# The opening of a fused kernel: loads, casts and residuals reordered across four engines

## The chip, the cores and the metric

The kernel runs on one core of one Trainium2 chip. The metric is the device time of one execution in microseconds; the profile's "span" is the time from the first to the last instruction of the profiled execution.

## The reference

```python
# x: 128 samples, 32 channels, 512 positions; all float32
def cond(x, c, weight, c_weight, bias):        # grouped convolution, 9 taps, 4 groups
    out = conv(x, weight, padding=4, groups=4)
    return out + (c @ c_weight.T)[:, :, None] + bias[None, :, None]

def ffn(y, base_W, base_b, router_W, router_b, A, B, expert_map):
    base_out = y @ base_W.T + base_b                       # 512 -> 512
    probs = softmax(y @ router_W.T + router_b)             # 15 routes
    topk_p, topk_i = top_k(probs, 8)
    w = sum of topk_p per expert, by expert_map[topk_i]    # 8 experts
    h = y @ A                                              # 8 experts x rank 16
    return base_out + ((h * w) @ B) * 2.0

out = x + ffn(cond(x, ...), ...)
```

## The kernel before

**Tiles.** The 4096 rows (sample, channel) of 512 positions are worked through as 32 tiles of 128 rows (4 samples, Q). Two tiles make a pair (8 samples), and the convolution is done by pairs, in two halves of 16 channels (`HALVES`); a unit is one half of one pair.

**Precision.** Every float32 operand of a matmul is split into a high part (`x_hi`, `wide_hi`, `y_hi`, `conv_hi`, a cast on ScalarE) and the residual (`x_lo`, `wide_lo`, ..., a subtraction on VectorE or GpSimd). A product is then three matmuls: high by high, the weight's residual by high, high by the data's residual. A residual reads two tensors in SBUF.

**Work of one tile t.** `conv` gives sums in PSUM; VectorE adds the conditioning (`condition`) and transposes (`turn`) into `y`; ScalarE casts (`y_high`); GpSimd makes `y_lo` (`y_low`). TensorE's `linear` multiplies y by the wide weights (`wide_sb`: 4 runs of 656 columns: A, router and base weights) into two PSUM banks, 400 columns in the first (FRONT_BANK) and 256 in the second. VectorE's `choose` (logits, best, top 8), `mark` and `weigh` make the routed hidden rows `hw`; TensorE turns `hw` (`turn_hw`), ScalarE and VectorE split it (`hw_high`, `hw_low`), TensorE's `up` adds it onto the sums, and VectorE's `add_out` adds x and the bias. `bias_rows` and `terms_low` are GpSimd's own work for each tile.

**Steps.** Every engine has its own function `step(t, k, p)` which is unrolled for the first 4 and last 8 tiles and looped between. In TensorE's step t the order is: front of `linear(t)`, `turn_hw(t-1)`, three runs of the second bank, `up(t-1)`, the last run, `conv(t)`. In VectorE's step t: `condition(t)`, `turn(t+2)`, `difference(t+5)`, `choose(t)`, `hw_low(t-1)`, `mark(t)`, `weigh(t)`, `add_out(t-1)`. The front of `linear(t)` waits for `out_added` of tile t-2, since it writes the same banks. Each engine executes its list in order, and a waiting instruction holds all behind it.

**Opening.** Tiles 0 to 3 (two pairs, `START`) don't use the looped convolution with its terms, but `conv_first` on plain blocks of x. The first pair is handled in its two tiles (a = 0, 1) and the second pair as a whole (`conv_second_pair`), after `linear(0)`. The first looped convolution, `conv(0)`, makes unit 4; its operands come from `difference`, `terms_high` and `terms_low`, and `conv_sum` is a weight that only it and its followers need. The tile `cond_sb` holds the conditioning; its weights come from HBM already repeated for each of the 8 output rows. `keep_warm` issues matmuls on zeros whose result nobody reads. DMAs are issued from SP's queue in the order written, apart from `conv_w` (ScalarE's) and the two that are read by all partitions, `expert_map` and `biases` (GpSimd's).

## Time and profile before

| | |
|---|---|
| time, median of 3 runs | 201.25 us (201.13 to 201.28) |
| the profiled execution's own time | 201.2 us |
| its span | 199.4 us |
| mean granted TensorE clock | 0.988 |
| TensorE busy | 189.7 us, 95% |
| VectorE busy | 163.1 us, 82% |
| GpSimd busy | 143.0 us, 72% |
| ScalarE busy | 76.5 us, 38% |

The profiled execution took 201.2 us, 1.8 us more than its span and 0.05 us less than the median. The busy times are sums over the whole span. All of the change lies in the opening, roughly the first 32 us, so the rows below are nearly all from there.

### The profile page before, as it was taken

Reading aid. Unit: us, or ns where it says so; the run is one execution under the profiler, and the core shown is the slowest. Engines: PE = TensorE matmul, PEld = TensorE weight load, DVE = VectorE, ACT = ScalarE, POOL = GpSimd, SP = SyncE. Lnnn points to the kernel's source line nnn. Section 1 sums busy time; section 2 is a strip of 40 time slices with the busy share of each in tenths; the row PEclk is TensorE's granted clock in tenths of the full one; section 3 lists DMA queues with packets and bytes.
Section 4 is the critical chain, followed back from the end, with each engine's and each line's share of the span. In section 5 each row is a group of like instructions: output and inputs, shape, how many; then the busy total and the mean of one; then the engine's idle time right before and its main releaser. Section 6 shows DMA issues by size and latency. Waiting matters only on the chain.

```text
span 199.4 us, 4327 instructions
## 1 busy us (share of the span) xinstructions
PE 189.7 (95%) x1300; PEld 181.7 (91%) x1300; DVE 163.1 (82%) x548; ACT 76.5 (38%) x196; POOL 143.0 (72%) x113
## 2 busy tenths in 40 slices
PE   7788699999999999999999999999999999998993
PEld 2667499999999999999999999999999999997992
DVE  1399898888898889898888889888988888775673
ACT  5164253444444343334444434333444443222210
POOL 5359989777777778877777777887777777943520
PEclk9999979999999999999999999999999999999998
DMA  7894054334445544434445544444343333333312
GB/s 168 281 393 161 16 144 141 119 121 133 130 159 165 159 159 139 144 117 135 131 130 156 159 159 159 137 146 121 125 153 118 100 105 108 105 105 110 105 53 105
DMA packets 18955, 27.78 MB, mean 139 GB/s; under 512 B 2112, under 2 KB 10176, under 8 KB 18944
## 3 DMA queue, kind: packets, MB, share of 16 engines
q1 hardware_dynamic: 18544, 26.98, 41.9%
q0 software_dynamic: 112, 0.28, 0.7%
q10 hardware_dynamic: 288, 0.39, 0.7%
q8 instruction: 5, 0.08, 0.2%
q14 instruction: 6, 0.05, 0.1%
HBM read 19.25 MB, written 8.39 MB: 139 GB/s over the span
## 4 chain that ended last, share of the span: by engine, by line
PE 83%; POOL 4%; DVE 4%; DMA 4%; issue 2%; ACT 1%; SPq 1%; DVEq 0%; ACTq 0%
PE wide_ps L496 54%; PE conv_banks L479 15%; PE wide_ps L520 10%; DMA x_in<-x_start 4%; POOL is_expert L430 2%; PE hwt_bank L507 2%; PE conv_banks L496 1%; POOL terms_lo L414 1%; DVE xr L612 1%; POOL y_lo L420 1%; DVE y_rows L617 1%; POOL map_f L427 0%; PE conv_banks L520 0%; DVE y L701 0%; SPq L251 0%
## 5 line engine op out<-in xcount | busy, mean ns | idle before, releaser
L496 PE MATMUL wide_ps<-wide_hi,y_hi 128*128 128x400 f32 (+1 forms) x248 | 80.8, 330 | 1.0 <-DVE xr L612 0.9
L496 PE MATMUL wide_ps<-wide_lo,y_hi 128*128 128x400 f32 (+1 forms) x248 | 76.6, 313 | 0.5 <-DVE wide_lo L221 0.5
L496 PE MATMUL wide_ps<-wide_hi,y_lo 128*128 128x400 f32 (+1 forms) x248 | 76.7, 314 | 0.0
L414 POOL TENSOR_TENSOR terms_lo<-terms,terms_hi 128x768 fp32r<-128x768 f32 x28 | 51.7, 1847 | 30.9 <-ACT terms_hi L336 30.9
L496 PEld LDWEIGHTS wide_ps<-wide_hi,y_hi 128*128 128x128 f32 x248 | 46.8, 190 | 3.5 <-issue 1.2
L496 PEld LDWEIGHTS wide_ps<-wide_lo,y_hi 128*128 128x128 f32 x248 | 46.8, 190 | 0.8 <-DVE wide_lo L221 0.8
L496 PEld LDWEIGHTS wide_ps<-wide_hi,y_lo 128*128 128x128 f32 x248 | 46.5, 189 | 0.0
L409 POOL TENSOR_TENSOR xr<-xr,biases_sb 128x512 f32<-128x512 f32 x32 | 41.5, 1296 | 6.2 <-DMA xr<-x_rows 6.2
L420 POOL TENSOR_TENSOR y_lo<-y,y_hi 128x512 fp32r<-128x512 f32 x32 | 41.4, 1293 | 3.3 <-ACT y_hi L343 3.3
L350 ACT ACTIVATE hw_hi<-hwt_bank 128x128 fp32r<-128x128 f32 x31 | 8.6, 278 | 82.5 <-PE hwt_bank L507 82.5
L343 ACT ACTIVATE y_hi<-y 128x512 fp32r<-128x512 f32 x32 | 20.3, 633 | 17.8 <-PE wide_ps L496 17.0
L479 PE MATMUL conv_banks<-terms_hi,conv_hi 128*128 128x256 f32 x84 | 23.7, 283 | 1.9 <-POOL terms_lo L414 1.9
L336 ACT ACTIVATE terms_hi<-terms 128x768 fp32r<-128x768 f32 x28 | 23.2, 829 | 2.6 <-DVE terms L642 2.6
L479 PE MATMUL conv_banks<-terms_lo,conv_hi 128*128 128x256 f32 x84 | 23.9, 285 | 0.0
L479 PE MATMUL conv_banks<-terms_hi,conv_lo 128*128 128x256 f32 x84 | 23.8, 283 | 0.0
L701 DVE STREAM_TRANSPOSE y<-y_rows 128x512 f32<-128x512 f32 x32 | 22.6, 708 | 1.1
L633 DVE TENSOR_TENSOR y_rows<-conv_banks,common 128x512 f32<-128x512 f32 x28 | 19.4, 692 | 2.9
L612 DVE TENSOR_TENSOR xr<-wide_ps,xr 128x512 f32<-128x512 f32 x30 | 20.4, 682 | 0.5 <-PE wide_ps L520 0.3
L642 DVE TENSOR_TENSOR terms<-even,odd_bank 128x256 f32<-128x256 f32 x56 | 20.0, 395 | 0.0
L479 PEld LDWEIGHTS conv_banks<-terms_hi,conv_hi 128*128 128x128 f32 x84 | 16.0, 191 | 2.3 <-issue 2.3
L479 PEld LDWEIGHTS conv_banks<-terms_hi,conv_lo 128*128 128x128 f32 x84 | 16.1, 191 | 0.0
L479 PEld LDWEIGHTS conv_banks<-terms_lo,conv_hi 128*128 128x128 f32 x84 | 16.0, 191 | 0.0
(93 smaller groups left out, 265.7 us busy)
## 6 DMA issues: line engine op xcount, KB each, us to landing
xr<-x_rows SPq DMA_DIRECT2D x32, 256.0 KB, 2.7
out<-xr SPq DMA_DIRECT2D x31, 256.0 KB, 2.0
even<-x_even SPq DMA_DIRECT2D x28, 132.0 KB, 2.5
...
```

What stands on the lines that cost most here:

```text
L336: nc.scalar.activation(terms_hi[i % 2][:, :, :, :], terms[i][:, :, :, :], ACT.Copy)\
L343: nc.scalar.activation(y_hi[k % 2][:, :, :], y[k % 2][:, :, :], ACT.Copy)\
L409: nc.gpsimd.tensor_tensor(xr[k][:, :], xr[k][:, :], base_b_sb[:, :], ALU.add)\
L414: nc.gpsimd.tensor_tensor(terms_lo[i % 2][:, :, :, :], terms[i][:, :, :, :], terms_hi[i % 2][:, :, :, :].bitcast(F32), ALU.subtract)\
L420: nc.gpsimd.tensor_tensor(y_lo[k % 2][:, :, :], y[k % 2][:, :, :], y_hi[k % 2][:, :, :].bitcast(F32), ALU.subtract)\
L479: mm = nc.tensor.matmul(sums, w[:, h, j, :], a[i][:, j, :, :], start=w is conv_hi and a is terms_hi, stop=a is terms_lo)
L496: mm = nc.tensor.matmul(sums_of(t, k)[:, b, 0:columns[1] - columns[0]], a[k % 2][:, r, :], w[:, r, columns[0]:columns[1]], start=r == 0 an ...
L520: mm = nc.tensor.matmul(sums_of(t, k)[:, b, first:first + HALF], a[k % 2][:, :], w[:, b * HALF:(b + 1) * HALF], start=False, stop=True, sk ...
L612: nc.vector.tensor_tensor(rows, linear_sums(t, k), rows, ALU.add)\
L633: nc.vector.tensor_tensor(y_rows[i][:, h, :, :].rearrange("p n (a k) -> p a n k", a=2), own_ps, common[:, :, :].unsqueeze(1).to_broadcast( ...
L642: d = nc.vector.tensor_tensor(terms[i][:, j, :, :], even[i][:, :, j:j + MK], odd_ps, ALU.subtract)
L701: nc.vector.transpose(y[k % 2][:, :, :].rearrange("p r (n h o) -> p h n r o", n=Q, h=HALVES), y_rows[(k // 2) % 2][:, :, own, :]).then_inc ...
```

## The change

The loads are issued in another order and in other pieces: the x blocks of tile 0, run 0 of the wide weights, the x blocks of tile 1, runs 1, 2 and 3, the second pair. `cond` goes to ScalarE's queue with 83 KB in place of 193 KB, and GpSimd repeats its weights for the 8 output rows. `biases` goes from GpSimd's queue to SP's. All x_hi of the opening are ScalarE's; x_lo of tile 0 stays with VectorE and those of tile 1 and the second pair go to GpSimd; all four wide_lo and y_lo of tile 0 are VectorE's; `is_expert` is one VectorE instruction in place of eight of GpSimd. `add_condition` writes its rows in order and reads PSUM with a step of two, where it read in order and wrote with a step. On VectorE, `choose`, `mark` and `weigh` of tile 0 now come ahead of the rows of the second pair, and `up_lo` after them; on TensorE, `conv(0)` now comes behind the front of `linear(1)`, and the three products of `conv_first` are issued in the order in which their operands come.

```diff
@@ sync
-            sync.dma_start(x_in[0][:, :, 0:Q, :], x_start[0, :, :, 0:Q, :])\
-                .then_inc(x_first_in, 16)
-            sync.dma_start(cond_in_sb[:, :], cond).then_inc(cond_in, 16)
-            sync.dma_start(x_in[0][:, :, Q:, :], x_start[0, :, :, Q:, :]).then_inc(x_second_in, 16)
-            for r in range(0, RUNS, 2):
-                sync.dma_start(wide_sb[:, r:r + 2, :], wide_w[:, r:r + 2, :])\
-                    .then_inc(wide_in[r // 2], 16)
-            sync.dma_start(x_in[1][:, :, :, :], x_start[1]).then_inc(x_third_in, 16)
+            sync.dma_start(x_in[0][:, :, :, :], x_first[0]).then_inc(x_loaded[0], 16)
+            load_wide(0)
+            sync.dma_start(x_in[1][:, :, :, :], x_first[1]).then_inc(x_loaded[1], 16)
+            load_wide(1)
+            load_wide(2)
+            load_wide(3)
+            sync.dma_start(x_in[2][:, :, :, :], x_pair).then_inc(x_loaded[2], 16)
             load_terms(0, 0)
+            sync.dma_start(biases_sb[:, :], biases.partition_broadcast(P)).then_inc(biases_in, 16)
+            load_terms(1, 1)
             sync.dma_start(up_sb[:, :], up_w).then_inc(up_in, 16)
-            load_terms(1, 1)
@@ tensor
+            for a in range(PAIR // Q):
+                sums = first_ps if a == 0 else conv_ps[:, :, Q:, :]
+                pe.wait_ge(x_hi_ready, a + 1)
+                for h in range(HALVES):
+                    conv_first(sums[:, h, :, :], a, h, (X_HIGH,))
                 for h in range(HALVES):
                     if a == 0:
                         pe.wait_ge(conv_lo_ready, h + 1)
+                    conv_first(sums[:, h, :, :], a, h, (X_W_REST,))
                 if a == 0:
                     ...
+                for h in range(HALVES):
+                    pe.wait_ge(x_lo_ready[a], h + 1)
+                    mm = conv_first(sums[:, h, :, :], a, h, (X_REST,))
+                mm.then_inc(first_done, 1)
@@ tensor, first_step and step
-                pe.wait_ge(y_lo_ready, 1)
+                for r in runs[:RUNS // 2]:
+                    pe.wait_ge(wide_lo_ready, r + 1)
+                    linear(0, 0, (r,), products=(W_REST,))
+                pe.wait_ge(y_lo_first, 1)
                 linear(0, 0, runs, products=(Y_REST,), last=(RUNS - 1, W_REST))
...
                     linear(t, k, runs, (FRONT_BANK,)).then_inc(front_done, 1)
+                    if isinstance(t, int) and t == 1:
+                        conv(0, 0, 0)
                     turn_hw(t - 1, k - 1)
@@ vector, add_condition
-                    rows.rearrange("p n (a k) -> p n k a", a=2),
-                    sums.rearrange("p n (k a) -> p n k a", a=2),
-                    c.unsqueeze(2).unsqueeze(3).to_broadcast([P, batches, MK, 2]), ALU.add)\
+                    rows.rearrange("p n (a k) -> p n a k", a=2),
+                    sums.rearrange("p n (k a) -> p n a k", a=2),
+                    c.unsqueeze(2).unsqueeze(3).to_broadcast([P, batches, 2, MK]), ALU.add)\
@@ vector, step 0
+                if isinstance(t, int) and t == 0:
+                    dve.wait_ge(up_hi_ready, 1)
+                    nc.vector.scalar_tensor_tensor(out=up_lo[:, :], in0=up_sb[:, :], ...)
+                    return
```

The lists below are the engines' programs in order, each instruction with its output, inputs and size. First VectorE in the opening, before: from the residual of tile 1's x blocks (`x_lo0`, here a part of the pair's tile) to the transpose of tile 2.

```order
L605 TENSOR_TENSOR x_lo0<-x_in0,x_hi0 128x2x260
L731 TENSOR_SCALAR cond_sb<-odd_bank,cond_in_sb 128x128 x2
L617 TENSOR_TENSOR y_rows0<-wide_ps0,cond_sb 128x4x32x2 x2
L701 STREAM_TRANSPOSE y0<-y_rows0 128x2x4x4x16
L617 TENSOR_TENSOR y_rows0<-conv_banks,cond_sb 128x4x32x2 x2
L701 STREAM_TRANSPOSE y1<-y_rows0 128x2x4x4x16
L221 TENSOR_TENSOR wide_lo<-wide_sb,wide_hi 128x656 x3
L743 SCALAR_TENSOR_TENSOR up_lo<-up_sb,up_hi 128x512
L605 TENSOR_TENSOR x_lo1<-x_in1,x_hi1 128x520 x2
L642 TENSOR_TENSOR terms0<-even0,odd_bank 128x256 x2
L617 TENSOR_TENSOR y_rows1<-conv_banks,cond_sb 128x8x32x2 x2
L701 STREAM_TRANSPOSE y0<-y_rows1 128x2x4x4x16
```

The same place after the change, from `wide_lo` of run 0 to the first operation of `choose`, tile 0 (`logits0`).

```order
L752 TENSOR_TENSOR wide_lo<-wide_sb,wide_hi 128x656
L766 TENSOR_TENSOR cond_sb<-odd_bank,cond_in_sb 128x256
L642 TENSOR_TENSOR y_rows0<-wide_ps0,cond_sb 128x256 x2
L726 STREAM_TRANSPOSE y0<-y_rows0 128x2x4x4x16
L752 TENSOR_TENSOR wide_lo<-wide_sb,wide_hi 128x656
L773 TENSOR_TENSOR y_lo0<-y0,y_hi0 128x512
L752 TENSOR_TENSOR wide_lo<-wide_sb,wide_hi 128x656 x2
L642 TENSOR_TENSOR y_rows0<-conv_banks,cond_sb 128x256 x2
L726 STREAM_TRANSPOSE y1<-y_rows0 128x2x4x4x16
L781 TENSOR_TENSOR is_expert<-map_f,expert_ids 128x120
L667 TENSOR_TENSOR terms0<-even0,odd_bank 128x256 x2
L674 TENSOR_TENSOR logits0<-wide_ps0,biases_sb 128x15
```

The two large x_lo and up_lo are gone from here, and a fourth wide_lo, y_lo0 and is_expert have come. The first wide_lo stands ahead of cond_sb and of tile 0's rows, and the logits of tile 0 stand ahead of y_rows1 (the second pair).

GpSimd from behind the memsets to the first bias rows, before:

```order
L397 DMA map_i<-expert_map 128x15
L399 TENSOR_TENSOR conv_sum<-conv_sb 128x256
L402 TENSOR_TENSOR conv_lo<-conv_sum,conv_hi 128x2x128
L405 DMA biases_sb<-biases 128x527
L221 TENSOR_TENSOR wide_lo<-wide_sb,wide_hi 128x656
L420 TENSOR_TENSOR y_lo0<-y0,y_hi0 128x512
L427 CAST map_f<-map_i 128x15
L430 TENSOR_SCALAR is_expert<-map_f 128x15 x8
L420 TENSOR_TENSOR y_lo1<-y1,y_hi1 128x512
L414 TENSOR_TENSOR terms_lo0<-terms0,terms_hi0 128x768
L409 TENSOR_TENSOR xr0<-xr0,biases_sb 128x512
```

and after:

```order
L406 DMA map_i<-expert_map 128x15
L408 MEMSET expert_ids 128x1 x8
L410 COPY cond_w_sb<-cond_in_sb 128x256
L224 TENSOR_TENSOR x_lo1<-x_in1,x_hi1 128x260 x2
L417 CAST map_f<-map_i 128x15
L419 TENSOR_TENSOR conv_sum<-conv_sb 128x256
L224 TENSOR_TENSOR x_lo2<-x_in2,x_hi2 128x520 x2
L438 TENSOR_TENSOR y_lo1<-y1,y_hi1 128x512
L445 TENSOR_TENSOR conv_lo<-conv_sum,conv_hi 128x2x128
L432 TENSOR_TENSOR terms_lo0<-terms0,terms_hi0 128x768
L427 TENSOR_TENSOR xr0<-xr0,biases_sb 128x512
```

GpSimd has lost wide_lo, y_lo0, eight is_expert and one DMA issue, and has got eight small memsets, the copy of the conditioning weights and four x_lo, two of 128x260 and two of 128x520.

ScalarE from the weight casts of the convolution on, before:

```order
L303 ACTIVATE conv_hi<-conv_sb 128x256 x2
L306 ACTIVATE conv_hi<-conv_sum 128x2x128
L309 ACTIVATE x_hi0<-x_in0 128x2x260
L315 ACTIVATE wide_hi<-wide_sb 128x656 x2
L343 ACTIVATE y_hi0<-y0 128x512
L315 ACTIVATE wide_hi<-wide_sb 128x656 x2
L357 ACTIVATE x_hi1<-x_in1 128x1040
L343 ACTIVATE y_hi1<-y1 128x512
L330 COPY odd_bank<-terms0 128x256
L362 ACTIVATE up_hi<-up_sb 128x512
```

and after:

```order
L309 ACTIVATE conv_hi<-conv_sb 128x256 x2
L313 ACTIVATE x_hi0<-x_in0 128x520
L319 ACTIVATE wide_hi<-wide_sb 128x656
L313 ACTIVATE x_hi1<-x_in1 128x520
L319 ACTIVATE wide_hi<-wide_sb 128x656 x2
L347 ACTIVATE y_hi0<-y0 128x512
L319 ACTIVATE wide_hi<-wide_sb 128x656
L313 ACTIVATE x_hi2<-x_in2 128x1040
L365 ACTIVATE conv_hi<-conv_sum 128x2x128
L334 COPY odd_bank<-terms0 128x256
L347 ACTIVATE y_hi1<-y1 128x512
```

The cast `wide_hi` of run 0 now stands between the casts of tile 0's and tile 1's x blocks, and the cast of conv_sum has moved behind all of them.

## Rows read from the trace of the kernel before

**Rows 1.** Windows: stretch, length, busy us of PE, PEld, DVE, ACT, POOL, PEclk, DMA share, GB/s.

```profile
4.00:6.00 2.00, 1.33 (x4) 0.15 (x1) 1.75 (x3) 0.62 (x2) 1.47 (x3) 1.00 0.96 112
8.00:10.00 2.00, 2.00 (x11) 1.85 (x9) 0.09 (x1) 0.64 (x1) 0.00 (x0) 1.00 1.01 416
24.06:27.47 3.41, 3.41 (x15) 3.39 (x14) 2.94 (x14) 1.96 (x5) 2.31 (x2) 0.50 0.59 155
60.00:115.00 55.00, 55.00 (x400) 54.35 (x399) 48.79 (x170) 22.82 (x60) 43.27 (x31) 1.00 0.47 144
```

**Rows 2.** Timeline, 20 to 33 us: start, us, engine, instruction [idle before <-releaser].

```profile
20.41 1.13 DVE L617 TENSOR_TENSOR y_rows<-conv_banks,cond_sb 128x512 f32<-128x512 f32 x1 [0.51 <-PE conv_banks L457]
...
21.83 1.05 DVE L617 TENSOR_TENSOR y_rows<-conv_banks,cond_sb 128x512 f32<-128x512 f32 x1 [0.28 <-PE conv_banks L457]
22.97 0.71 DVE L701 STREAM_TRANSPOSE y<-y_rows 128x512 f32<-128x512 f32 x1
...
23.66 0.36 PE L479 MATMUL conv_banks<-terms_hi,conv_hi 128*128 128x256 f32 x1 [1.87 <-POOL terms_lo L414]
...
24.24 0.16 DVE L649 TENSOR_TENSOR logits<-wide_ps,biases_sb 128x15 f32<-128x15 f32 x1
...
25.35 0.28 DVE L673 TENSOR_TENSOR spread<-is_expert,wide_ps 128x120 f32<-128x120 f32 x1
...
26.33 0.41 DVE L628 TENSOR_TENSOR common<-conv_banks,cond_sb 128x256 f32<-128x256 f32 x1
...
26.85 0.69 DVE L633 TENSOR_TENSOR y_rows<-conv_banks,common 128x512 f32<-128x512 f32 x1
...
27.46 0.70 DVE L701 STREAM_TRANSPOSE y<-y_rows 128x512 f32<-128x512 f32 x1
...
29.22 0.29 DVE L712 TENSOR_TENSOR hw_lo<-hwt_bank,hw_hi 128x128 fp32r<-128x128 f32 x1
...
31.16 0.69 DVE L612 TENSOR_TENSOR xr<-wide_ps,xr 128x512 f32<-128x512 f32 x1 [0.19 <-issue]
...
32.00 0.42 PE L496 MATMUL wide_ps<-wide_hi,y_hi 128*128 128x400 f32 x1
```

**Rows 3.** Timeline, 9 to 20 us.

```profile
9.24 0.64 ACT L309 ACTIVATE x_hi<-x_in 128x520 fp32r<-128x520 f32 x1 [4.53 <-DMA x_in<-x_start]
9.91 0.70 DVE L605 TENSOR_TENSOR x_lo<-x_in,x_hi 128x520 fp32r<-128x520 f32 x1 [3.32 <-ACT x_hi L309]
10.53 0.60 DVE L731 TENSOR_SCALAR cond_sb<-odd_bank,cond_in_sb 128x128 f32<-128x128 f32 x2
...
10.89 1.40 ACT L315 ACTIVATE wide_hi<-wide_sb 128x656 fp32r<-128x656 f32 x2 [1.01 <-DMA wide_sb<-wide_w]
...
11.16 1.13 DVE L617 TENSOR_TENSOR y_rows<-wide_ps,cond_sb 128x256 f32<-128x256 f32 x2
...
17.94 1.30 DVE L605 TENSOR_TENSOR x_lo<-x_in,x_hi 128x520 fp32r<-128x520 f32 x2
```

**Rows 4.** Timeline, 3 to 14 us, GpSimd.

```profile
3.54 0.72 POOL L399 TENSOR_TENSOR conv_sum<-conv_sb 128x256 f32<-128x256 f32 x1 [0.62 <-DMA conv_sb<-conv_w]
...
4.79 1.18 POOL L402 TENSOR_TENSOR conv_lo<-conv_sum,conv_hi 128x256 fp32r<-128x256 f32 x1 [0.53 <-ACT conv_hi L306]
...
13.78 1.30 POOL L420 TENSOR_TENSOR y_lo<-y,y_hi 128x512 fp32r<-128x512 f32 x1 [0.47 <-ACT y_hi L343]
```

**Rows 5.** Instructions of lines L724, L221 and L315: ns min/median/max, first and last start.

```profile
L724 DVE TENSOR_TENSOR conv_lo<-conv_sb,conv_hi x2: 412/680/947, 5.3 to 6.2; 128x256 fp32r<-128x256 f32 x2
...
L221 DVE TENSOR_TENSOR wide_lo<-wide_sb,wide_hi x3: 828/829/1097, 14.7 to 16.4; 128x656 fp32r<-128x656 f32 x3
...
L315 ACT ACTIVATE wide_hi<-wide_sb x4: 736/738/754, 10.9 to 14.3; 128x656 fp32r<-128x656 f32 x4
```

**Rows 6.** Tiles wide_sb, then map_i: from issue to landing, min/median/max.

```profile
DMA to landing us min/median/max: 8.2/9.0/9.9
...
DMA to landing us min/median/max: 6.5/6.5/6.5
```

More of the change, by code:

```diff
@@ L131, in build @@
         cond_in = sem("cond_in")
-        wide_in = [sem(f"wide_in{i}") for i in range(RUNS // 2)]
+        cond_w_ready = sem("cond_w_ready")
+        wide_in = [sem(f"wide_in{i}") for i in range(RUNS)]
         up_in = sem("up_in")
@@ L176, in build @@
         y_hi_ready = sem("y_hi_ready")
+        y_lo_first = sem("y_lo_first")
         y_lo_ready = sem("y_lo_ready")
@@ L421, in y_low @@
                                         y_hi[k % 2][:, :, :].bitcast(F32), ALU.subtract)\
[L422 to L432 removed]
+                    .then_inc(y_lo_ready, tiles)
+            y_low(1, 1, 2)
+            pool.wait_ge(conv_sum_hi_ready, 1)
+            nc.gpsimd.tensor_tensor(conv_lo[:, :, BLOCKS, :], conv_sum[:, :, :],
+                                    conv_hi[:, :, BLOCKS, :].bitcast(F32), ALU.subtract)\
+                .then_inc(conv_sum_lo_ready, 1)
             terms_low(FIRST_UNIT, 0)
@@ L484, in conv @@
                 mm.then_inc(conv_done, 1)
+            X_HIGH, X_W_REST, X_REST = (conv_hi, x_hi), (conv_lo, x_hi), (conv_hi, x_lo)
             FRONT_BANK, NEXT_BANK = 0, 1
@@ L740, in _ @@
                 turn(a, a)
-            split_wide(dve, nc.vector, range(1, RUNS))
-            dve.wait_ge(up_hi_ready, 1)
-            nc.vector.scalar_tensor_tensor(out=up_lo[:, :], in0=up_sb[:, :], scalar=LORA_SCALE,
-                                           in1=up_hi[:, :].bitcast(F32), op0=ALU.mult,
-                                           op1=ALU.subtract).then_inc(up_lo_ready, 1)
-            dve.wait_ge(x_hi_ready, 2)
-            for h in range(HALVES):
-                x_low_first(1, (every, h, every, every))
-            difference(FIRST_UNIT, 0)
+            wide_low(0)
+            dve.wait_ge(cond_summed, 1)
+            nc.vector.tensor_tensor(cond_sb[:, :, :], cond_ps,
+                                    conv_b_sb.unsqueeze(2).to_broadcast([P, HALVES, N]), ALU.add)\
+                .then_inc(cond_biased, 1)
+            dve.wait_ge(cond_biased, 1)
+            first_rows(0, first_ps)
+            wide_low(1)
+            dve.wait_ge(y_hi_ready, 1)
+            nc.vector.tensor_tensor(y_lo[0][:, :, :], y[0][:, :, :],
+                                    y_hi[0][:, :, :].bitcast(F32), ALU.subtract)\
+                .then_inc(y_lo_first, 1)
+            wide_low(2)
+            wide_low(3)
+            first_rows(1, conv_ps[:, :, Q:, :])
+            dve.wait_ge(map_ready, 1)
+            dve.wait_ge(ids_ready, E)
+            nc.vector.tensor_tensor(is_expert[:, :, :],
+                                    map_f[:, :].unsqueeze(1).to_broadcast([P, E, ROUTES]),
+                                    expert_ids[:, :].unsqueeze(2).to_broadcast([P, E, ROUTES]),
+                                    ALU.is_equal).then_inc(is_expert_ready, 1)
+            difference(FIRST_UNIT, 0)
+            dve.wait_ge(biases_in, 16)
+            choose(0, 0)
+            mark(0, 0)
+            dve.wait_ge(is_expert_ready, 1)
+            weigh(0, 0)
             for h in range(HALVES):
@@ L805 @@
     blocks = blocks.reshape(N // PAIR, P, HALVES, PAIR, MI)
+    first = blocks[0].reshape(P, HALVES, 2, Q, MI).transpose(2, 0, 1, 3, 4)
     units = blocks[START:].transpose(0, 2, 1, 3, 4).reshape(-1, P, PAIR, MI)
@@ L831 @@
     given = {
-        "x_start": blocks[:START],
+        "x_first": first,
+        "x_pair": blocks[1],
         "x_even": units[..., 0::2],
```

170 lines of the change are left out of this document (83 added, 87 removed).

## The prediction

> **What bounds the kernel now.** The page's totals (the table above) have TensorE busy for 95% of the span and VectorE for 82%. Next the windows: from 60 to 115 us TensorE is busy for 55.00 of 55 us at full clock [rows 1]. The change leaves those steps alone, so a gain must show as an earlier start of the steady part. As its mark I take the start of linear(2), 32.00 us [rows 2]; 167.4 us of the span follow it.
>
> What ends last before that mark is read from the timeline, backwards. TensorE starts linear(2) at 32.00, right behind VectorE's add_out of tile 0 (31.16 + 0.69 = 31.85) [rows 2]. That in turn ends an unbroken list of VectorE: common of step 1 starts at 26.33, hw_lo at 29.22, add_out at 31.16. TensorE looks worse off than VectorE: it waited 1.87 us for terms_lo before conv(0) at 23.66 [rows 2], and ran at half clock from 24.06 to 27.47 [rows 1]. But both were hidden, for VectorE reached the logits of tile 0 only at 24.24 and common at 26.33. So the path is VectorE's list from 9.91 (x_lo of tile 1, released by a cast at 9.24, released by a DMA [rows 3]) to 26.33: 16.42 us, in which it idled only 0.51 + 0.28 = 0.79 us, for the sums of the second pair (ahead of 20.41 and 21.83 [rows 2]). I call the start of common of step 1 C1. Before, C1 = 26.33 and linear(2) = C1 + 5.67.
>
> **The change on VectorE's list, in costs from start to start.**
> - Gone: x_lo of tile 1, 10.53 - 9.91 = 0.62; x_lo of the second pair, 1.22 for two (17.94 onwards; 1.30 busy, the next starts 0.08 before the end as elsewhere [rows 3]). Sum 1.84.
> - Gone: the waits of 0.79. The routes of tile 0 now stand there, 26.33 - 24.24 = 2.09 [rows 2], and cover them. Without that cover they would be back.
> - cond_sb: 11.16 - 10.53 = 0.63 [rows 3] becomes one instruction of 256 columns from PSUM like common, 26.85 - 26.33 = 0.52 [rows 2]. Saves 0.11.
> - add_condition: two of 128x256 took 1.13 us [rows 3], so four some 2.25; the two of 128x512 took 1.13 and 22.97 - 21.83 = 1.14 [rows 2]. Instructions from PSUM that write in order take 0.41 for 256 columns (common) and 27.46 - 26.85 = 0.61 for 512 [rows 2]. No row shows a read of PSUM with a step. Bounds: as now, saving 0, or as those. I take the second, nearest in all else: (2.25 - 4 x 0.41) + (2.27 - 2 x 0.61) = 0.61 + 1.05 = 1.66.
> - Added: wide_lo of run 0, 0.83 (the median [rows 5]); y_lo of tile 0, 0.64 (512 columns are 0.69 busy, as in add_out, less the same overlap); is_expert, 0.28, as the 120-column spread [rows 2]. Sum 1.75. up_lo, the differences and the transposes only change place.
>
> **The price of giving x_lo to GpSimd.** Conv_lo is twice the same instruction on VectorE and took 412 and 947 ns [rows 5]; the long one ran while GpSimd was in its own conv_lo, 4.79 to 5.97, which took 1.18 us, where conv_sum of the same size took 0.72 [rows 4]. The longest wide_lo, 1097 ns against 828, was the first, from 14.7 [rows 5], while GpSimd's y_lo ran until 13.78 + 1.30 = 15.08 [rows 4]. So these two engines hold each other up when each reads two SBUF tensors. After the change, x_lo of the second pair (two of about 1.30 us, as y_lo of like size [rows 4]) comes up for GpSimd near 15 us, amid wide_lo 2 and 3 on VectorE. Bounds: nothing, if VectorE always comes first; 2.5 us, if both halves do. I take one half, for the two queues should alternate: 1.20 us. The loss of 0.27 in a wide_lo is kept, now against conv_sum.
>
> The Trainium skill (SBUF — State Buffer, "Who interferes with whom") says that VectorE with two SBUF inputs and GpSimd reading SBUF fully block each other, whoever issues first. That speaks against this edit. Where the rows alone, taken as each engine losing half of an overlap, would charge 0.6 us here, by the rule it is a whole GpSimd instruction, or two.
>
> Sum: 16.42 - 1.84 - 0.79 - 0.11 - 1.66 + 1.75 + 1.20 = 14.97 us from the start of the list to C1.
>
> **When the list starts.** wide_lo of run 0 is first, so it waits for run 0's DMA and cast. The DMAs are crippled early: 112 GB/s in 4 to 6 us at a busy share of 0.96, 416 GB/s in 8 to 10 [rows 1]. Meanwhile the small map_i load is out, 6.5 us on its way [rows 6]; it stays where it is. The second x piece landed at 9.2, the first wide piece at 10.9 [rows 3]. Up to the second x piece 256 + 260 + 193 + 260 = 969 KB were asked for; up to run 0 it will be 256 + 83 + 260 + 328 = 927 KB. The 42 KB are 0.1 us at 416 GB/s, so run 0 lands at about 9.1; its cast takes 0.74 [rows 5] and the list starts at 9.87, almost as before. Bounds: without the slow stretch 927 KB at 416 GB/s from the 2 us at which data begins to flow would land at 4.4; at the other end 11.4, below.
>
> C1 = 9.87 + 14.97 = 24.84, against 26.33.
>
> **What else could hold C1?** Following the same costs down the list, wide_lo 3 ends at 17.3, tile 1's rows at 18.1 and its transpose at 18.7, and the routes at 21.9. TensorE does the second pair's matmuls behind those rows and is done by 21, within the routes. Conv(0) needs terms_lo: ScalarE's y_hi1 19.4, then GpSimd's y_lo1 20.7, conv_lo (0.7 to 1.2) 21.6, terms_lo (1.8) 23.4; its first part is done at 23.8, 1 us to spare. hw_lo follows C1 by 2.89 us as before, for the same steps precede it [rows 2]. TensorE will idle at up(0) instead, 1.5 to 2.5 us that cost nothing by themselves. So linear(2) = 24.84 + 5.67 = 30.51. The span becomes 197.9, the profiled time 199.7, and against the median 201.25 - 1.49 = **199.75 us**. The keep_warm matmuls ahead of linear(0) (7, now 4) lie where TensorE waits for y_hi of tile 0 and count for nothing; without that wait fewer could only help.
>
> **The rivals.**
> - *The clock.* Before, a half-clock stretch of 3.41 us [rows 1] followed TensorE's wait of 1.87 us [rows 2]. After the change such a wait stands at up(0), about 25.5 to 27.7. The stretch costs half of itself, 1.7 us of work; some 0.85 us is free between the end of conv(1) and linear(2). So 0.85 us is paid if it falls before that mark, 1.7 at most if across it: 200.6, at worst 201.45. For it: this wait. Against: it is broken by up(0)'s first products. Chance 0.2.
> - *The rows stay dear.* If a read with a step costs as much as the write did, 1.66 us of the gain goes: 201.4, no change. Chance 0.12.
> - *The slow DMA stretch shrinks.* If run 0 lands a us or more earlier, the list starts as much earlier, until later weights bind: 198.0 to 198.8. Chance 0.15. For it: VectorE's cast of tile 0's x, at 4.2, falls into the slow stretch and goes. Against: map_i goes out as before. The Trainium skill (SBUF — State Buffer, "SBUF: two separate sides") says that a float32 copy on VectorE keeps GpSimd from writing the descriptors of its own DMA; by that rule map_i would be over sooner. No row here separates this.
> - *Slower: run 0 lands late.* A wide piece took up to 9.9 us from issue [rows 6]. Issued second, at about 1.5, run 0 would then land at 11.4, 2.3 us later than I take; as it stands ahead of cond_sb, all of VectorE's list moves: 199.75 + 2.3 = 202.05. It decides from a landing after 11.0. For it: it lies in the slow stretch. Against: only small loads are ahead of it. Chance 0.12; other losses that end above 201.65 (both halves of x_lo ahead of wide_lo together with half clock) 0.08.
> - The forecast, 199.1 to 200.4, has the remaining 0.33.
>
> **Numbers.** The range for 8 in 10 reaches from the early landing, 198.1, to a little past the late one's threshold, 201.9. About 0.2%, or 0.4 us, is what this kernel's timing can tell from no change. Faster by more: the forecast 0.33, the early DMA 0.15, most of the clock's 0.2 (0.15): 0.63. Same: 0.12 + 0.05 = 0.17. Slower: 0.20.
>
> **What would show it.** C1, the first common, near 24.8; linear(2) near 30.5; wide_lo of run 0 beginning near 9.9 with VectorE idle ahead of it; y_rows at 0.41 and 0.69 us; one of the last two wide_lo lengthened by about 1.2 us beside GpSimd's x_lo; no gap on VectorE between that and C1; TensorE waiting at up(0). The forecast is wrong if VectorE is not what linear(2) waits for, if run 0 lands far from 9.1, or if the granted clock is 0.5 when linear(2) starts.

## The result, and the profile after

The changed kernel takes 198.26 us in the median of 4 runs (197.58 to 198.88), the kernel before 201.26 beside it: ratio 0.985, 95% interval 0.981 to 0.988. The gain is 3.0 us where 1.5 were forecast; 198.26 lies at the lower edge of the range (198.1 to 201.9), and in size it is the rival "the slow DMA stretch shrinks": its condition, run 0 landing a us or more earlier, came true, though the stretch did not shrink. The same kernel measured once more (e18 below) took 197.70 (197.46 to 198.00) beside 201.37.

VectorE's list in the opening, in the timeline of the profiled execution (start, duration, in brackets the idle time ahead and what ended it). These rows answer to [rows 2, 3].

```profile
6.91 0.83 DVE L752 TENSOR_TENSOR wide_lo<-wide_sb,wide_hi 128x656 fp32r<-128x656 f32 x1
9.05 0.42 DVE L766 TENSOR_TENSOR cond_sb<-odd_bank,cond_in_sb 128x256 f32<-128x256 f32 x1 [1.32 <-PE odd_bank L557]
9.98 0.76 DVE L642 TENSOR_TENSOR y_rows<-wide_ps,cond_sb 128x256 f32<-128x256 f32 x2 [0.50 <-PE wide_ps L471]
...
11.41 0.80 DVE L752 TENSOR_TENSOR wide_lo<-wide_sb,wide_hi 128x656 fp32r<-128x656 f32 x1
12.18 0.69 DVE L773 TENSOR_TENSOR y_lo<-y,y_hi 128x512 fp32r<-128x512 f32 x1
12.79 1.59 DVE L752 TENSOR_TENSOR wide_lo<-wide_sb,wide_hi 128x656 fp32r<-128x656 f32 x2
...
15.71 1.24 DVE L781 TENSOR_TENSOR is_expert<-map_f,expert_ids 128x120 f32<-128x120 f32 x1
...
19.70 1.28 DVE L642 TENSOR_TENSOR y_rows<-conv_banks,cond_sb 128x512 f32<-128x512 f32 x2
...
22.88 0.41 DVE L653 TENSOR_TENSOR common<-conv_banks,cond_sb 128x256 f32<-128x256 f32 x1
```

C1, the start of `common` of step 1, is at 22.88 us, 3.45 earlier than the 26.33 of before [rows 2]. Two things differ from the forecast's list at its head: wide_lo of run 0 is long done, and VectorE then idles 1.32 and 0.50 us for TensorE. GpSimd beside it:

```profile
7.29 1.74 POOL L224 TENSOR_TENSOR x_lo<-x_in,x_hi 128x260 fp32r<-128x260 f32 x2 [0.92 <-ACT x_hi L313]
...
13.93 2.89 POOL L224 TENSOR_TENSOR x_lo<-x_in,x_hi 128x520 fp32r<-128x520 f32 x2 [3.15 <-ACT x_hi L313]
```

TensorE's timeline: first convolution, then from up(0) to linear(2).

```profile
1.32 4.02 PE L465 MATMUL wide_ps<-zeros 128*128 128x512 bf16 x9 [1.32 <-POOL zeros L400]
6.09 1.22 PE L471 MATMUL wide_ps<-x_hi,conv_hi 128*128 128x256 f32 x4 [0.74 <-ACT x_hi L313]
7.11 1.05 PE L471 MATMUL wide_ps<-x_hi,conv_lo 128*128 128x256 f32 x4
7.96 1.05 PE L557 MATMUL odd_bank<-cond_in_sb,cond_w_sb 128*128 128x128 f32 x4
...
24.38 0.48 PE L535 MATMUL wide_ps<-up_hi,hw_hi 128*128 128x256 f32 x2 [0.75 <-ACT hw_hi L354]
...
26.09 0.50 PE L535 MATMUL wide_ps<-up_hi,hw_lo 128*128 128x256 f32 x2 [1.00 <-DVE hw_lo L737]
...
27.37 0.42 PE L493 MATMUL conv_banks<-terms_hi,conv_lo 128*128 128x256 f32 x1
27.59 0.41 PE L493 MATMUL conv_banks<-terms_lo,conv_hi 128*128 128x256 f32 x1
...
28.52 0.67 PE L511 MATMUL wide_ps<-wide_hi,y_hi 128*128 128x400 f32 x1
```

Linear(2) starts at 28.52, C1 + 5.64 (before: + 5.67). But the span is 197.1, so 168.6 us follow it where 167.4 did before. The windows show why, and how the loads fared; the last three columns are granted clock, DMA share and GB/s, as in [rows 1].

```profile
4.00:6.00 2.00, 1.35 (x4) 0.16 (x2) 0.76 (x2) 1.21 (x4) 0.04 (x1) 1.00 1.06 393
6.00:8.00 2.00, 1.91 (x9) 1.91 (x10) 1.67 (x3) 1.20 (x3) 1.08 (x2) 1.00 0.97 148
8.00:10.00 2.00, 2.00 (x11) 2.00 (x11) 0.44 (x2) 0.32 (x1) 1.15 (x3) 1.00 0.93 359
...
26.00:28.00 2.00, 1.91 (x12) 1.91 (x13) 1.63 (x9) 1.67 (x4) 2.00 (x3) 0.77 0.50 141
28.00:30.00 2.00, 2.00 (x9) 1.84 (x8) 1.86 (x4) 0.00 (x0) 2.00 (x2) 0.50 0.36 135
```

The slow DMA stretch did not go: it came at 6 to 8 us (148 GB/s) instead of 4 to 6 (112 [rows 1]). Run 0 landed ahead of it, at 5.74, and the second x piece as it began, at 6.48 (ScalarE casts them at 5.94 and 6.58 without a wait); run 1 landed behind it, at 9.66. Two signs that the forecast had named against itself are there: run 0 landed far from 9.1, and the granted clock was 0.5 when linear(2) started.

### The profile page after: what moved, and what is told of

It reads as the page before. It is cut to its first block, busy times and chain, and to the rows that moved or that the text cites. A ratio compares the mean times of both kernels' runs of the same rounds, so it can differ in the third digit from the quotient of the medians.

```text
span 197.1 us, 4329 instructions
## 1 busy us (share of the span) xinstructions
PE 189.0 (96%) x1297; PEld 181.9 (92%) x1297; DVE 161.1 (82%) x547; ACT 77.0 (39%) x197; POOL 139.4 (71%) x115
## 4 chain that ended last, share of the span: by engine, by line
PE 84%; DVE 9%; issue 2%; DMA 2%; ACT 1%; DVEq 0%; ACTq 0%
PE wide_ps L511 53%; PE conv_banks L493 15%; PE wide_ps L535 10%; DMA conv_sb<-conv_w 2%; PE hwt_bank L522 2%; PE wide_ps L471 1%; PE conv_banks L511 1%; DVE y_rows L642 1%; DVE wide_lo L752 1%; DVE y L726 1%; DVE terms L667 1%; DVE xr L637 1%; DVE spread L698 0%; DVE expert_w L702 0%; PE odd_bank L557 0%
## 5 line engine op out<-in xcount | busy, mean ns | idle before, releaser
L438 POOL TENSOR_TENSOR y_lo<-y,y_hi 128x512 fp32r<-128x512 f32 x31 | 40.2, 1296 | 3.4 <-ACT y_hi L347 3.4
```

The costliest lines, as they stand in the source:

```text
L438: nc.gpsimd.tensor_tensor(y_lo[k % 2][:, :, :], y[k % 2][:, :, :], y_hi[k % 2][:, :, :].bitcast(F32), ALU.subtract)\
```

## The experiments

There are eighteen runs; C1 and the start of the first y_rows are from each profiled execution. The kernel before measured 201.0 to 201.4 us in the medians beside them, so that differences under some 0.4 us between rows of the table are not shown by the times alone; the ratio is to the kernel before beside the run.

| run | time, us (range) | ratio, 95% interval | first y_rows | C1 |
|---|---|---|---|---|
| before | 201.26 | 1 | 11.16 | 26.33 |
| changed | 198.26 (197.58-198.88) | 0.981-0.988 | 9.98 | 22.88 |
| e1 run 0 behind x | 197.96 (197.55-198.37) | 0.980-0.986 | 8.20 | 23.02 |
| e5 map first | 197.41 (196.91-197.87) | 0.977-0.984 | 9.89 | 22.79 |
| e9 warm-up 10 | 197.93 (197.44-198.60) | 0.981-0.988 | 8.22 | 22.69 |
| e17 cond last | 197.97 (197.28-199.03) | 0.980-0.986 | 8.60 | 22.33 |
| e18 changed again | 197.70 (197.46-198.00) | 0.979-0.984 | 8.11 | 22.87 |
| e4 before, new loads | 201.84 (201.33-202.28) | 1.001-1.004 | 11.88 | 27.14 |
| e6 before, map late | 200.71 (199.77-200.83) | 0.994-0.998 | 10.79 | 25.91 |
| e14 before, rows | 200.99 (200.34-201.36) | 0.997-1.001 | 11.04 | 25.55 |
| e15 before, rows and routes | 199.30 (198.93-199.84) | 0.988-0.994 | 11.37 | 24.39 |
| e2 old rows | 199.12 (198.15-199.70) | 0.983-0.991 | 9.87 | 23.88 |
| e10 pair on VectorE | 199.68 (198.62-200.02) | 0.986-0.993 | 9.97 | 24.18 |
| e11 rows ahead of routes | 199.63 (199.48-199.90) | 0.989-0.994 | 8.24 | 24.66 |
| e7 is_expert early | 197.33 (196.95-198.40) | 0.978-0.984 | 9.73 | 22.40 |
| e8 warm at up(0) | 197.29 (197.19-197.55) | 0.978-0.984 | 8.00 | 22.15 |
| e3 map late | 196.67 (196.12-198.82) | 0.974-0.986 | 8.03 | 21.08 |
| e12 together | 198.01 (197.92-198.47) | 0.982-0.987 | 8.17 | 22.87 |
| e13 together, second | 197.14 (196.92-197.24) | 0.977-0.983 | 8.18 | 21.91 |
| e16 map late, warm | 196.36 (196.22-196.66) | 0.973-0.980 | 8.10 | 21.17 |

**What sets the head of the list.** e1 swaps two loads of the changed kernel, e4 gives the kernel before the new order of loads.

```diff
 e1
-            load_wide(0)
             sync.dma_start(x_in[1][:, :, :, :], x_first[1]).then_inc(x_loaded[1], 16)
+            load_wide(0)
 e4: x piece 1, run 0, x piece 2, runs 1 to 3 one by one; cond on ScalarE's queue
```

> The changed kernel with one edit: run 0 of the weights is issued behind the second x piece instead of ahead of it. Theory (the list's head): the gain beyond the forecast came from run 0 landing before the slow DMA stretch. Behind it, run 0 lands when run 1 did, at about 9.7 us; its cast ends at 10.4, wide_lo of run 0 starts at 10.45 and cond_sb at 11.3 instead of 9.05, so the first common goes from 22.88 to about 25 and the time from 198.3 to about 200.4. Rival (the list itself got shorter, its head does not matter): the first common moves by under 0.5 us and the time by under 0.5.

> The kernel before with the changed kernel's load order only (run 0 second, then the second x piece, each run by itself, cond on ScalarE's queue). Theory (the load order alone brings the early start): the second x piece lands by 7 us instead of 9.2, x_lo of tile 1 starts near 7.3 instead of 9.91, and the first y_rows come at about 10 instead of 11.16, held by TensorE's first matmuls; the first common comes 1.2 to 1.6 us earlier and the time is 199.7 to 200.2. Rival (the early landing is owed to something else in the change, as to what GpSimd or VectorE do in the opening): x and run 0 land as late as before and the time stays at 201.2.

Both expectations failed, and so did the reading that the place of run 0 in the queue matters. In e1 run 0 still landed as the slow stretch began (cast at 6.20). In e4 it landed in the stretch, at 7.09, and the second x piece behind it: ScalarE waited 5.11 us and cast the piece at 9.96, later than before. Up to that piece e4 asks for 256 + 260 + 328 + 260 + 193 = 1297 KB, the changed kernel, with 83 KB of cond, for 1187. That is 0.3 us at 400 GB/s and does not by itself explain 3.5 us. The issue times on SyncE's queue say more (before and e4, then the changed kernel; GpSimd issues expert_map at 2.17 or 2.16 in all three):

```profile
2.08 0.55 SPq L254 DMA_DIRECT2D x_in<-x_start  x1
2.08 0.55 SPq L256 DMA_DIRECT2D x_in<-x_start  x1
1.66 0.42 SPq L264 DMA_DIRECT2D x_in<-x_first  x1
```

The second x piece, issued at 2.08, landed at 9.22 and 9.94; issued at 1.66 it landed at 6.48. Run 1 of the changed kernel, issued at 2.13, landed at 9.66. So what was issued 0.5 us or more ahead of expert_map came in ahead of the stretch or in it, and what was issued within 0.1 us of it came behind. In the changed kernel one issue follows the other every 0.44 to 0.47 us, before and in e4 every 0.59 to 0.73. No run changes the issue times alone, so this is what the traces agree on and not shown as the cause. e5 and e6 move the load of expert_map, which I suspected of making the stretch:

```diff
 e5
             nc.gpsimd.memset(zeros[:, :], 0.0).then_inc(zeros_ready, 1)
+            pool.dma_start(map_i[:, :], expert_map.partition_broadcast(P)).then_inc(map_in, 16)
 e6, in before.py, behind the load of x_in[1]
+            sync.dma_start(map_i[:, :], expert_map.partition_broadcast(P)).then_inc(map_in, 16)
```

> The changed kernel with the small load of expert_map issued about 1 us earlier, as GpSimd's second instruction. Theory (that load makes the slow DMA stretch, and the stretch comes where the load stands among the loads issued): the slow stretch begins before 5 us instead of at about 6, the second x piece and run 0 land in or behind it as in the kernel before (after 7.5 us), the first common is 24 or later instead of 22.9 and the time 199.2 to 200.5. Rival (the stretch comes at a set time after the loads begin, whatever the order): it stays at 6 to 8 us and the time stays within 0.5 us of the changed kernel's 198.3.

> The kernel before with the load of expert_map issued by SyncE behind the second pair's x, nothing else. Theory (the kernel before lost its start to the slow DMA stretch): no slow stretch; the second x piece lands near 5.5 us instead of 9.2; TensorE's first matmuls, from 6.4, then set the pace, so the first y_rows come at 8.5 to 9.7 instead of 11.16; the first common comes 1.5 to 2.5 us earlier than 26.33 and the time falls to 198.8 to 199.8. Rival (other loads or engines hold the list anyway, as when run pairs land late): under 0.8 us gained.

The windows of e5 have the stretch a us earlier:

```profile
5.00:6.00 1.00, 0.35 (x2) 0.01 (x1) 0.79 (x3) 1.00 (x4) 0.17 (x1) 1.00 0.82 74
6.00:7.00 1.00, 1.00 (x4) 1.00 (x5) 1.00 (x3) 0.58 (x1) 0.23 (x1) 1.00 0.77 252
```

So the first half of the theory stands: the stretch follows that load. The packets of GpSimd's queue agree: they begin at 4.4 us before, 5.2 in e4, 5.8 in the changed kernel and 4.9 in e5, and the stretch begins with them; why they came later in the changed kernel than before, from the same issue time, stays open. The theory's price does not stand: the second x piece was cast at 7.52 instead of 6.58, and C1 stayed (22.79). e6 has no stretch there and gained 0.4 us of C1, not 1.5 to 2.5. Its timeline says what else held the kernel before:

```profile
7.11 0.70 DVE L605 TENSOR_TENSOR x_lo<-x_in,x_hi 128x520 fp32r<-128x520 f32 x1 [0.57 <-ACT x_hi L310]
10.14 0.61 DVE L731 TENSOR_SCALAR cond_sb<-odd_bank,cond_in_sb 128x128 f32<-128x128 f32 x2 [2.33 <-PE odd_bank L540]
```

The x_lo came 2.8 us earlier than before and was followed by a wait of 2.33 for TensorE, whose cond matmuls stood behind tile 0's twelve products. e9 and e17 look at TensorE itself.

```diff
 e9
-WARM_UP, WARM_BETWEEN = 9, 4
+WARM_UP, WARM_BETWEEN = 10, 4
 e17: the cond matmuls behind the loop over X_REST instead of ahead of it
```

> The changed kernel with 10 instead of 9 matmuls on zeros ahead of the first convolution (they end at about 5.8 us instead of 5.34, when x_hi of tile 0 is ready). Theory (the head of VectorE's list is set by TensorE's first matmuls, which ran at half speed, 0.28 instead of 0.16 us each, after a pause of 0.5 to 0.7 us): they run at full speed, cond_sb starts at 7.5 to 7.9 instead of 9.05 and the first y_rows at 8.2 instead of 9.98; then the list waits for run 1 of the weights, and the first common is at 22.2 to 23.0; time 0 to 0.7 us lower. Rival (the head is set by the loads): cond_sb stays near 9.

> The changed kernel with the matmuls for cond behind all of tile 0's products, as in the kernel before, instead of ahead of the x_lo products. Theory (TensorE's order sets the head of VectorE's list): where TensorE's first matmuls run at half speed, cond_sb starts at 10.0 to 10.2 instead of 9.05 and the first y_rows at 10.6 instead of 9.98, and the first common comes 0.6 us later, 23.5; where they run at full speed the list waits for run 1 of the weights anyway and nothing changes; time +0.2 to +0.6. Rival (the order is indifferent): no change within 0.2 us.

> The changed kernel unaltered. Expected 198.0 to 198.5 in the median, as before; runs whose mean clock is 0.991 about 1 us longer than runs with 0.998 or more, if the half-clock stretch falls on the path, and first common at 22.0 to 23.0.

The first convolution comes at two speeds. In the changed kernel's profile its 256-column matmuls follow each other every 0.21 us (7.11 to 7.96 for four); e5, e7, e10, e2, e6, e14, e15 and the kernel before have the same, and all other runs have 0.12. These are the two levels of the clock. The matmuls on zeros of 512 columns ahead of it follow every 0.43 us, and every 0.22 after 11.3 us; the step of the 256-column matmuls falls from 0.21 to 0.12 at 10.07; and 0.21 us is also the step between 27.37 and 27.59 above, where the granted clock is 0.50, against 0.12 in e18 at the same place at 1.00. The windows' 1.00 ahead of 10 us says nothing here: the trace's record of the granted clock begins only with a first entry of 1.00, at 10.02 us in the changed kernel and 9.65 to 10.41 in all the runs with 0.21, but at 3.97 to 6.04 in all the runs with 0.12, and where there is no entry 1.00 is filled in. So TensorE began at the lower level, and rose during the matmuls on zeros or within 1 us behind them in some executions, and only at 10 us, in the products of tile 1's blocks, in others of the same kernel. e18 is the changed kernel at the fast one (its median, 197.70, is 0.3 us under what was expected of it):

```profile
8.11 0.76 DVE L642 TENSOR_TENSOR y_rows<-wide_ps,cond_sb 128x256 f32<-128x256 f32 x2
8.90 0.71 DVE L726 STREAM_TRANSPOSE y<-y_rows 128x512 f32<-128x512 f32 x1
10.85 0.84 DVE L752 TENSOR_TENSOR wide_lo<-wide_sb,wide_hi 128x656 fp32r<-128x656 f32 x1 [1.23 <-ACT wide_hi L319]
```

The first rows come 1.87 us earlier, and the list then stands 1.23 us (and 0.49 ahead of y_lo) until run 1 has landed behind the slow stretch: C1 is 22.87 against 22.88. In the five runs at the fast speed with this list C1 is run 1's landing plus 12.8 to 12.9 us (9.33 and 22.15 in e8, 9.47 and 22.33 in e17, 9.82 and 22.69 in e9, 10.04 and 22.87 in e18, 10.20 and 23.02 in e1); at the slow speed, in the changed kernel and e5, it is the first y_rows plus 12.90. So two limits meet in the changed kernel, TensorE's slow start and run 1's landing, and taking one away (e1, e5, e9, e18) leaves C1 within 22.7 to 23.0. Since e18 has the fast speed with 9 matmuls on zeros, e9 does not show that a tenth brings it. e17 ran at the fast speed: with the cond matmuls last, the first y_rows came at 8.60 instead of 8.11, and C1 did not depend on it. That the same order is worth some 0.8 us at the slow speed (the cond matmuls begin 1.87 us after TensorE's first in the changed kernel, 2.70 in e6) stays argued, not shown.

**What the list is worth, term by term.** e2 undoes add_condition, e14 and e15 add parts of the change to the kernel before (e15 also moves ScalarE's exponentials of tile 0, which `choose` needs, ahead of terms_high).

```diff
 e2 (e14 is its reverse in before.py)
-                    rows.rearrange("p n (a k) -> p n a k", a=2),
-                    sums.rearrange("p n (k a) -> p n a k", a=2),
+                    rows.rearrange("p n (a k) -> p n k a", a=2),
+                    sums.rearrange("p n (k a) -> p n k a", a=2),
 e15: e14, and ahead of the pair's rows on VectorE
+            choose(0, 0)
+            mark(0, 0)
+            weigh(0, 0)
```

> The changed kernel with the old add_condition (step in the write instead of in the read). Theory (the rows' price was a term of the list): y_rows take about 0.57 us (256 columns) and 1.13 us (512) instead of 0.395 and 0.64, the first common comes 1.6 us later, about 24.5, and the time is 199.3 to 199.9. Rival (after the change TensorE's half-clock stretch, not VectorE's list, decides linear(2)): the rows are as dear, but the time rises by under 0.6 us.

> The kernel before with the changed add_condition only (step in the read of PSUM, not in the write). Theory: y_rows take 0.76 instead of 1.13 us for two of 256 columns and 0.68 instead of 1.13 for one of 512; the 0.75 us of tile 0 and 1's rows count in full, of the pair's 0.9 us half is lost to a longer wait for TensorE's sums of the second half; first common at 25.0 to 25.4 instead of 26.33, time 200.0 to 200.4. Rival (without waits it all counts): first common 24.7, time 199.6. Rival (the list before was held elsewhere, by TensorE or the weights): under 0.4 us gained.

> The kernel before with the changed add_condition and the routes of tile 0 ahead of the second pair's rows. Theory (the routes cover VectorE's waits for the pair's sums): the 0.79 us of waits and the rest of the rows' gain come in, first common at 24.0 to 24.3, time 199.0 to 199.4, that is about 1 us under the rows alone. Rival (conv(0), which waits for terms_lo and stands ahead of linear(1) on TensorE, then holds the first common): no better than the rows alone.

In e2 the rows took 1.13 and 2.01 us (two each) instead of 0.76 and 1.28: 1.5 us, of which C1 lost only 1.00 (1.6 were expected), since is_expert waited 0.4 less. In e14 the waits for the pair's sums were 0.51 and 0.72 us (0.51 and 0.28 before [rows 2]), as expected, and C1 gained 0.78, less than expected; the time's gain, 0.3 us, is not clear of its interval. In e15 the waits are gone, C1 is at 24.39, 1.94 ahead of before, and the time is 2.0 us under the kernel before beside it. Rows and routes alone thus bring 2.0 of the 3.0 us. e11 and e10 undo parts of the changed kernel's list.

```diff
 e10, behind tile 1's transpose (and gone from GpSimd)
+            for h in range(HALVES):
+                x_low(nc.vector, 2, h)
 e11: choose, mark and weigh of tile 0 behind the add_condition of y_rows[1]
 e7: the wait for map_ready and is_expert directly ahead of wide_low(2)
```

> The changed kernel with x_lo of the second pair back on VectorE, behind tile 1's transpose. By the prediction's terms this gives back 1.22 us of list and takes away a price of 1.20: no change. By what the traces show since, the price was 0.96 (is_expert 1.24 instead of 0.28), so the first common comes 0.3 us later, 0.8 if TensorE's second pair, now waiting for it, makes the rows of the pair late; time 0.2 to 0.8 us higher than the changed kernel's. Rival (the lock moves on to the next VectorE instruction with a large read, as up_lo): more than 1 us later.

> The changed kernel with the routes of tile 0 (logits to hw) back behind the rows of the second pair. Theory (the routes cover the waits for the pair's sums): VectorE is ready for the rows at 17.5, TensorE's sums are done at about 17.4 and 18.8, so one wait of 0.5 to 0.7 us appears between the two y_rows; the first common comes that much later, 23.4 to 23.6, time +0.4 to +0.7. Rival (the order is free, as conv(0) or other work holds the first common): no change within 0.2.

> The changed kernel with VectorE's is_expert moved ahead of the third wide_lo, where GpSimd idles (10.8 to 13.9 us). Theory A (the long is_expert, 1.24 us, is the lock by GpSimd's x_lo of the second pair, and only instructions with two SBUF inputs are caught): is_expert takes 0.28, all behind it comes 0.9 us earlier, first common near 22.0, time 0.5 to 0.9 lower. Theory B (whatever reads SBUF next pays): the difference (one SBUF, one PSUM input) or the last wide_lo, which now slides towards x_lo, takes the 0.9 us and the first common stays at 22.9 within 0.3.

"The lock" stands for VectorE and GpSimd holding each other up at work in SBUF: is_expert took 1.24 us beside GpSimd's x_lo in the changed kernel, and 0.28 in e7, where GpSimd idled. e10: C1 is 1.30 us later, 1.19 for the two x_lo and 0.13 for is_expert, which took 1.37 us though GpSimd no longer had the pair's x_lo; it was in y_lo of tile 1 (16.59 to 18.12). So the lock is not the price of the hand-over, and the expected 0.3 to 0.8 us failed. e11 shows the wait that the routes cover, and another lock that was not expected:

```profile
18.92 0.69 DVE L642 TENSOR_TENSOR y_rows<-conv_banks,cond_sb 128x512 f32<-128x512 f32 x1 [0.74 <-PE conv_banks L471]
...
22.95 1.79 DVE L805 SCALAR_TENSOR_TENSOR up_lo<-up_sb,up_hi 128x512 fp32r<-128x512 f32 x1
```

0.74 us of wait and 1.12 that up_lo took longer (1.79 against 0.67 in the changed kernel) make C1 1.78 later, where 0.5 to 0.7 were expected. e7 (expectation above) moves is_expert ahead of the third wide_lo, where GpSimd idles: it took 0.28 us, but up_lo 1.27, so 0.60 of the 0.96 saved was paid there; C1 is 22.40, between the two theories.

**The half clock.** e8 puts matmuls on zeros into TensorE's two waits at up(0).

```diff
+                if isinstance(t, int) and t == 0:
+                    keep_warm_up(5)            # 256 columns of wide_ps[1][:, 1, HALF:]
                 pe.wait_ge(hw_hi_ready, t + 1)
...
+                            keep_warm_up(8)
                             pe.wait_ge(hw_lo_ready, t + 1)
```

> The changed kernel with matmuls on zeros in TensorE's two waits of step 1: 5 of 256 columns ahead of the wait for hw_hi (0.75 us idle), 8 ahead of the wait for hw_lo (1.00 us idle). Theory (those two waits bring the half-clock stretch at 27 us, which costs some 0.9 us when it comes): granted clock 1.00 from 20 to 40 us in every run, so span clock above 0.995 in all of them, and a median 0.5 to 0.9 us lower. Rival (the stretch has another cause, or costs nothing because VectorE is the path): the granted clock still falls in some runs, or the time stays within 0.3 us.

```profile
24.13 1.05 PE L469 MATMUL wide_ps<-zeros 128*128 128x256 bf16 x8
25.36 0.50 PE L544 MATMUL wide_ps<-up_hi,hw_lo 128*128 128x256 f32 x2 [0.18 <-DVE hw_lo L746]
```

The idle time of 1.00 us is 0.18, and all four runs have a mean clock of 1.00. The median is 0.4 us under that of e18, but that is not shown to be the edit's: the kernel before beside it was 0.4 lower too (201.01 against 201.37), and in the profile C1 was already 0.72 earlier, by run 1's landing. Against an execution at full clock the matmuls gain nothing (167.7 us behind the start of linear(2) in both); what they may save is the half clock. Of the nine runs of the changed kernel and e18, the four at a mean clock of 0.991 take 198.27 on average, the five at 0.998 or more 197.74; but three of the four are from the first set, and the one of e18, 197.68, is no longer than its fellows. The profiles say it more clearly: 168.6 us follow the start of linear(2) at 28.52, against 196.2 - 28.51 = 167.7 in e18. e7, which has the stretch too, has 168.6. In e10 and e2 it fell ahead of linear(2), which then started at C1 + 6.33 and + 6.37 instead of + 5.64. So it costs 0.7 to 0.9 us when it comes behind C1; before and in e6 and e11, where it began ahead of C1, it cost 0.2 at most by the same two measures (start of linear(2) behind C1, span behind linear(2)).

**Taking the losses away.**

```diff
 e3 (GpSimd's load of map_i is gone)
             sync.dma_start(x_in[2][:, :, :, :], x_pair).then_inc(x_loaded[2], 16)
+            sync.dma_start(map_i[:, :], expert_map.partition_broadcast(P)).then_inc(map_in, 16)
 e16: e3 with the matmuls of e8 (2 and 12)
 e12: e16 with 10 warm-up matmuls, the cast of map_i and is_expert behind wide_low(3) on VectorE
 e13: map_i behind x_in[1] instead, is_expert as in e7, the matmuls of e8 (2 and 12)
```

> The changed kernel with the small load of expert_map taken from GpSimd's queue and issued by SyncE behind the second pair's x. Theory (that small load slows all DMA queues while it is out): no stretch of 2 us under 250 GB/s is left between 4 and 10 us, and runs 1 to 3 and the second pair land 1.5 us or more earlier; the time falls by 0 to 0.5 us, since cond_sb waits for TensorE, or rises by up to 1 if map_f then holds up GpSimd. Rival (the slow stretch has another cause): the 6 to 8 us window stays under 200 GB/s and run 1 still lands at 9.7.

> The changed kernel with four edits together: the load of expert_map on SyncE behind the second pair's x (no slow DMA stretch), its cast and is_expert on VectorE behind the last wide_lo (no work of GpSimd beside it), 10 matmuls on zeros at the start, and matmuls on zeros in step 1 while TensorE waits for hw_hi (2) and hw_lo (12). Theory: the first common at 20.3 to 20.8, no half clock in any run, linear(2) at about 26.2, span about 193.7, time 195.3 to 195.8. Rival (up_lo or another instruction takes over the lock with GpSimd, and GpSimd's terms_lo is late): the first common at 21.1 as with the map alone, time 196.0 to 196.4.

> The changed kernel with the load of expert_map on SyncE behind the second x piece, is_expert ahead of the third wide_lo (GpSimd idle), and matmuls on zeros in step 1's two waits (2 and 12). Theory (three separate losses that add up: slow DMA stretch, lock, half clock): no slow stretch, is_expert 0.28 us, first common at 20.3 to 20.8, no half clock, linear(2) at 26.0 to 26.4, time 195.1 to 195.7. Rival (up_lo takes the lock over, 1.3 to 1.8 us long): first common at 21.1, time 195.9 to 196.4.

> The changed kernel with the load of expert_map on SyncE behind the second pair's x, and the matmuls on zeros in step 1's waits (2 and 12). Theory: first common at 21.1 as with the map alone, granted clock 1.00 in every run, and no run near 198.8, time 195.9 to 196.4. Rival (the run at 198.82 with the map alone had another cause, as it had full clock): such runs come again.

Windows of e3, then of e13, whose map load, also on SyncE's queue, is issued behind the second x piece:

```profile
6.00:8.00 2.00, 2.00 (x19) 2.00 (x19) 1.76 (x4) 1.82 (x4) 1.04 (x2) 1.00 1.06 412
```

```profile
6.00:7.00 1.00, 1.00 (x9) 1.00 (x10) 1.00 (x3) 1.00 (x2) 0.15 (x1) 1.00 0.27 40
```

In e3 the loads run at 412 GB/s where the changed kernel had 148, run 1 lands at 6.93 instead of 9.66, and the slow time is at 9 to 12 us (166 to 206 GB/s), when the weights are in: C1 is 21.08 and the time 1.6 us under the changed kernel's (1.0 under e18's), where 0 to 0.5 were expected. In e13 it is back at 6 us, 40 GB/s, and the list again waits for run 1, which landed at 9.45. So it is this load that slows the others, on GpSimd's queue or SyncE's, and it does so where it stands among them. e12 lost its gain to the lock, on VectorE:

```profile
12.48 1.29 DVE L786 CAST map_f<-map_i 128x15 f32<-128x15 int32 x1
13.80 1.33 DVE L789 TENSOR_TENSOR is_expert<-map_f,expert_ids 128x120 f32<-128x120 f32 x1
```

GpSimd was in the two x_lo of the pair from 12.02 to 14.99, and each small instruction lasted about as long as one of them. e12 and e13 thus missed their expected times by over 1 us. e16, the best version, came within its own: it is 1.3 us under e18 and 4.96 under the kernel before beside it. Its C1 is that of e3, and its median is 0.3 us lower, within e3's spread; e3's one run at 198.82, at a mean clock of 1.00, did not come again in its four and stays unexplained.

## Why the prediction was off

- **The failed step is "When the list starts".** It had run 0 land at 9.1 us, because the slow stretch stayed at 4 to 6 us, and wide_lo of run 0 and cond_sb follow: first y_rows at 9.87 + 0.83 + 0.52 = 11.22. Measured 9.98, 1.24 us of the 1.96 by which C1 beats the forecast. It compared bytes ahead of the piece and held the stretch at its place. The stretch came 2 us later, run 0 landed at 5.74, its wide_lo cost nothing, and TensorE at its lower clock was the head. The forecast named TensorE's first matmuls nowhere, though before they were within 0.4 us of the x piece: the cond matmuls were done at 9.10 + 1.05 = 10.15, and cond_sb began at 10.53. The rival that had the early landing priced it right (198.0 to 198.8), with its "until later weights bind": e18 starts its rows at 8.11 and waits for run 1. Its cause was a shrunken stretch, and the stretch moved.
- **From the first rows to C1**: forecast 24.84 - 11.22 = 13.62, measured 12.90. The price of the lock, 1.20, was taken for the hand-over of x_lo and put on a wide_lo; it was 0.96 and fell on is_expert. The 0.27 kept for the first wide_lo was not paid (0.80). That is 0.51 of the 0.72; the rest is spread over the list. The mechanism of the lock was right, its place and its cause in the hand-over were not.
- **Rows and waits** were 2.45 (1.66 + 0.79); e15 gives 1.94 with a head 0.21 later, so 2.15. The 0.30 that are missing are in the three wide_lo, which took 2.92 us there instead of 2.60 before. The instruction costs were right (0.395 for 256 columns and 0.655 for 512 from start to start, where 0.41 and 0.61 were taken), and the cover by the routes is shown by e11. That a step in the read costs nothing is right: e2, with the step in the write, took 1.5 us more for the same rows. The rival of dear rows is out.
- **x_lo of the pair**, 1.22: e10 gives 1.19.
- **The clock** was a rival at 0.2 with 0.85 us: by the mean clock of 0.991 the half-clock stretch came in 4 of 9 runs, from 27.1 to 30.5 us in the profile, and cost 0.7 to 0.9 us by the profiles. Without it the miss would have been larger by as much, so the median of 198.26 owes its place inside the range to it in part. Against what the forecast held against it, up(0)'s first products between the two waits did not prevent it.
- The Trainium skill (SBUF — State Buffer, "Who interferes with whom") has a VectorE instruction with two SBUF inputs shut out for the whole of a GpSimd instruction that reads SBUF. The trace agrees: is_expert 0.28 us alone (e7), 1.24 to 1.37 beside GpSimd. The forecast's second reading of it, that the work to be moved decides the price, is what failed: whatever VectorE instruction of this kind comes while GpSimd is busy pays (is_expert, and up_lo in e3, e7, e11 and e13). The cast of 15 columns in e12 reads one SBUF tensor and took 1.29 us, so not only instructions with two inputs are caught here.
